# Layer 0's softmax maxima: one sequence of steps, half a pair ahead, in a fused two-layer decoder kernel

## The reference, cut to what matters

```
q = (x @ Wq).reshape(B, Nq, HEADS, DIM_HEAD)
k = (context @ Wk).reshape(B, context.shape[1], HEADS, DIM_HEAD)
v = (context @ Wv).reshape(B, context.shape[1], HEADS, DIM_HEAD)
sim = jnp.einsum('bihd,bjhd->bhij', q, k) * SCALE
attn = jax.nn.softmax(sim, axis=-1)
out = jnp.einsum('bhij,bjhd->bihd', attn, v)
```

## Time and profile before

| | |
|---|---|
| median of 3 runs | 1639.65 us (1639.27 to 1640.0) |
| the profiled execution | 1638.51 us, its span 1636.8 us |
| busy share of the span | PE 93%, DVE 79%, ACT 69%, POOL 30% |
| pair 0's maxima, alone | 59.6 to 125.1 us |
| slots of layer 0 | 130.0 to 1000.2 us |
| granted TensorE clock | 0.964 of full speed over the span |

### The profile page before, as it was taken

The page is one execution under the profiler, slowest core; times in us unless marked ns, Lnnn a source line. Parts: engine busy times, 40 slices in busy tenths (PEclk is TensorE's granted clock), DMA queues, the critical chain, the costliest instruction groups (busy, mean ns, idle before and its releaser), DMA issues.

```text
span 1636.8 us, 27033 instructions
## 1 busy us (share of the span) xinstructions
PE 1530.1 (93%) x9058; PEld 548.9 (34%) x9058; DVE 1286.3 (79%) x2319; ACT 1126.0 (69%) x1541; POOL 490.9 (30%) x488
## 2 busy tenths in 40 slices
PE   6889999999999999999999998899997979999986
PEld 4312333333333333333333223344444612222223
DVE  6898987879977779878789897877775666787766
ACT  6787777768877778777777786655554469676643
POOL 6303343334543334433300010345451012233100
PEclk9759999999999999999999998999999979999998
DMA  4000000000200000000010000111100000000000
GB/s 135 7 1 11 1 1 1 1 2 11 54 1 2 1 1 1 3 1 11 20 32 3 1 1 19 37 46 45 45 27 1 1 1 2 0 1 1 1 14 13
DMA packets 14834, 22.79 MB, mean 14 GB/s; under 512 B 1990, under 2 KB 11766, under 8 KB 14710
## 3 DMA queue, kind: packets, MB, share of 16 engines
q1 hardware_dynamic: 14710, 21.22, 4.6%
HBM read 20.69 MB, written 0.52 MB: 13 GB/s over the span
## 4 chain that ended last, share of the span: by engine, by line
PE 69%; issue 11%; DVE 9%; POOL 5%; ACT 4%; DMA 0%; POOLq 0%; SPq 0%; DVEq 0%; ACTq 0%
PE PS L2167 22%; PE PS L2153 15%; PE PS L2511 6%; PE PS L2199 5%; POOL WRK L734 5%; PE PS L2498 3%; DVE KNB L1382 3%; PE PS L2020 2%; PE PS L2012 2%; PE PS L2116 2%; PE PS L2540 2%; PE PS L2450 1%; PE PS L2435 1%; PE PS L2004 1%; ACT KNB L959 1%
## 5 line engine op out<-in xcount | busy, mean ns | idle before, releaser
L1382 DVE CUSTOM_DVE_ANT_0 KNB<-PS,KNB 128x512 f16<-128x512 f32 (+2 forms) x500 | 338.5, 690 | 152.4 <-PE PS L2199 106.9
L1432 DVE TENSOR_TENSOR WRK<-WRK 128x768 f32<-128x768 f32 (+3 forms) x400 | 425.2, 1063 | 15.3 <-ACT WRK L933 8.4
L933 ACT ACTIVATE WRK<-PS 128x1024 f32<-128x1024 f32 (+1 forms) x408 | 401.4, 1022 | 47.6 <-PE PS L2153 39.2
L2167 PE MATMUL PS<-WRK,V 128*64 128x512 f32 (+1 forms) x1632 | 395.7, 605 | 0.0
L708 POOL TENSOR_TENSOR WRK<-WRK 128x256 f32<-128x256 f32 x300 | 274.7, 916 | 395.6 <-ACT WRK L933 394.6
L959 ACT ACTIVATE KNB<-PS 128x512 f16<-128x512 f32 (+2 forms) x306 | 180.9, 591 | 77.8 <-PE PS L2199 77.2
L2344 PE MATMUL PS<-WRK,KNB 128*128 128x512 f16 x828 | 188.3, 381 | 7.1 <-POOL WRK L734 2.7
L2167 PEld LDWEIGHTS PS<-WRK,V 128*64 128x64 f32 (+1 forms) x1632 | 99.3, 136 | 192.7 <-issue 154.5
L2153 PE MATMUL PS<-KNB,KB 64*128 64x512 f16 (+1 forms) x1224 | 156.5, 377 | 0.0
L2153 PE MATMUL PS<-Q,KB 64*128 64x512 f16 (+1 forms) x1224 | 153.0, 377 | 0.0
L1162 ACT ACTIVATE WRK<-PS 128x1024 f32<-128x1024 f32 x100 | 102.4, 1024 | 51.1 <-PE PS L2498 47.6
(11 more groups left out here) (379 smaller groups left out, 1834.2 us busy)
## 6 DMA issues: line engine op xcount, KB each, us to landing
V<-in_moe_w_dram SPq DMA_DIRECT2D x44, 192.0 KB, 2.4
KNB<-in_ctx_fm_dram SPq DMA_DIRECT2D x6, 384.0 KB, 8.4
X<-in_ctx_fm_dram SPq DMA_DIRECT2D x12, 192.0 KB, 2.4
CTX<-in_ctx_fm_dram SPq DMA_DIRECT2D x6, 384.0 KB, 3.9
BW<-in_bit_w_dram SPq DMA_DIRECT2D x1, 960.0 KB, 9.8
PWK<-in_pair_w_dram SPq DMA_DIRECT2D x4, 192.0 KB, 2.8
XT<-in_x_fm_dram SPq DMA_DIRECT2D x1, 512.0 KB, 5.0
X<-in_x_tm_dram SPq DMA_DIRECT2D x1, 512.0 KB, 12.0
```

The source lines that it names most:

```text
L933: e.activation(PR[0:r, u % 2, b, :], bank(2 * b, 2 * b + 2, slice(0, r)), ACT.Exp).then_inc(S("exp"), 1)
L1382: return e.tensor_tensor_reduce(diffs, sums, diffs, 0.5, NEG, ALU.add, ALU.max, accum_out=out)
L1432: e.tensor_tensor(total, total, part, ALU.add).then_inc(S("acc"), 1)
L2167: ins = e.matmul(PS[h * HD:(h + 1) * HD, 4, :], V[0:r, j, h * HD:(h + 1) * HD], PR[0:r, unit_no(hf, i) % 2, b, h * HALF:(h + 1) * HALF], s ...
```

## The change

The steps become one sequence of 364 over the whole loop (`NSTEP`), 52 for each half from half 1 to half 7 (`NM`), each half's made on their own. Only half 0's maxima are found alone: 24 double steps and 2 short ones. The sequence starts in pair 0's slot 0 and goes through every slot, across the pairs' ends, two steps a slot with a third in slots 32, 34, 36, 38, 40, 42, 44, 48 and 50 of pairs 0 to 2 and in slots 3, 4 and 5 of pair 0. It ends in pair 3's slot 11, which has the last half step. The halves are complete in slots 24 and 47 of pair 0, 20 and 43 of pair 1, 15 and 39 of pair 2, and 11 of pair 3. In the slot behind each of these VectorE reduces that half's maxima and makes its two diagonal tiles, at the slot's start (`shifts`, which now holds what `diagonals` did).

A pair's `K16` chunks overwrite the ones before as soon as the half that reads them is through: slots `K16_AT` for `kd`, one later for `ks`. Queries, chunks and all else go through bank 5; `q` moves to slots 1 and 2. GpSimd also takes its quarter of the sums in half 6 (`POOL_HALVES`), makes the chain's first largest value ahead of that half and the second in its midst. The chain's first rounded copy goes to another tile (`KA[1]`), since `K16` is still read. The chain has one more empty item in front, so that its items stay in the same slots. The core of the diff:

```diff
-THIRD_M = (32, 36, 40, 44, 48)
...
+TILES_H = NT // 2
+STEPS = [[(c, [t], g) for c in range(NFULL) for t in range(TILES_H * u, TILES_H * u + TILES_H) for g in range(2)]
+         + [(NFULL, list(range(TILES_H * u + a, TILES_H * u + b)), g) for a, b in ((0, 3), (3, TILES_H)) for g in range(2)] for u in range(2)]
+NM = len(STEPS[0])
...
+ALONE0 = [(d, [t], g) for d in range(NDC - 1) for t in range(TILES_H) for g in range(2)] + [(NDC - 1, [0, 1, 2, 3], g)
+                                                                                     for g in range(2)]
...
+POOL_HALVES = 2 * PAIRS - 1
...
+NSTEP = NM * (2 * PAIRS - 1)
+WITH_VALUES = (32, 34, 36, 38, 40, 42, 44, 48, 50)
+THIRD_M = [(3, 4, 5) + WITH_VALUES] + [WITH_VALUES] * (PAIRS - 2) + [()]
+
+
+def first_step(p, s):
+    return min(2 * (p * SLOTS + s) + sum(len(x) for x in THIRD_M[:p]) + sum(t < s for t in THIRD_M[p]), NSTEP + 1)
...
+K16_AT = (6, 9, 13, 16, 20, 23, 25)
...
-        at[0] += [("wk", n), ("q", (n, 0)), ("q", (n, 1))]
-        at[1] += [("wv", n), ("kd", (n, 0)), ("ks", (n, 0))]
-        for c in range(1, NMC):
-            at[4 + 3 * c].append(("kd", (n, c)))
-            at[5 + 3 * c].append(("ks", (n, c)))
+        at[0].append(("wk", n))
+        at[1] += [("wv", n), ("q", (n, 0))]
+        at[2].append(("q", (n, 1)))
+        for c, k in enumerate(K16_AT):
+            at[k].append(("kd", (n, c)))
+            at[k + 1].append(("ks", (n, c)))
...
-CHAIN = [("none",)] * 2
+CHAIN = [("none",)] * 3
...
-        EMB = [KN[0].bitcast(BF16), KN[1].bitcast(BF16), KN[0].bitcast(BF16)]
+        EMB = [KA[1][:, :].bitcast(BF16), KN[1].bitcast(BF16), KN[0].bitcast(BF16)]
...
+            for hf in range(POOL_HALVES):
+                if hf == POOL_HALVES - 1:
+                    largest(0)
                 for i in range(NU):
                     for b in tiles_of(i):
                         add_up(hf, i, b)
-            for i in range(3):
-                e.wait_ge(S("ax"), i + 1)
-                e.partition_all_reduce(AM[:, i:i + 1], AX[:, i:i + 1], P, RED.max).then_inc(S("am"), 1)
+                    if hf == POOL_HALVES - 1 and i == CHAIN.index(("max", 1)) - 1:
+                        largest(1)
+            largest(2)
...
+            def shifts(hf, done, parts):
+
+                u, rows = hf % 2, slice(hf % 2 * NT, hf % 2 * NT + NT)
                 e.wait_ge(S("mx"), done)
-                link(e.tensor_reduce(NEGM[:, 0:rows], MXP[:, 0:rows, 0:parts], X, ALU.max, negate=True))
...
+                link(e.tensor_reduce(NEGM[:, rows], MXP[:, rows, 0:parts], X, ALU.max, negate=True))
+                if hf >= 2:
+                    e.wait_ge(S("sc"), tile_no(hf - 2, 0, 0) + 1)
+                for h in range(2):
+                    row = u * NT + h * TILES_H
                     ins = e.tensor_tensor(DIAG[:, h, 4 * u:4 * u + 4, :],
                                           ident16[:, :].unsqueeze(1).to_broadcast([P, 4, P]),
                                           NEGM[:, row:row + 4].unsqueeze(2).to_broadcast([P, 4, P]), ALU.mult)
                 ins.then_inc(S("diag"), 1)
...
-                    first, mid, last = split_steps(s) if p + 1 < PAIRS else ([], [], [])
-                    if s == SLOTS - 1 and p + 1 < PAIRS:
-                        shifts(micro_base(p + 1), NMC, 2 * NT)
-                        e.wait_ge(S("sc"), tile_no(2 * p, 0, 0) + 1)
-                        diagonals(0, 2, NT)
+                    first, mid, last = split_steps(p, s)
+                    if ready(p, s):
+                        shifts(ready(p, s), STEP0 + ready(p, s) * NM, NMC)
```

More of the change, by code:

```diff
@@ L93, in rows_of, with micro_steps, half_step, step @@
     return P if j < KT - 1 else TAIL
-THIRD_M = (32, 36, 40, 44, 48)
[L100 to L112, removed]
+NSTEP = NM * (2 * PAIRS - 1)
[3 more added lines that the diff above has]
+    return min(2 * (p * SLOTS + s) + sum(len(x) for x in THIRD_M[:p]) + sum(t < s for t in THIRD_M[p]), NSTEP + 1)
+def micro_steps(p, s):
+    return list(range(first_step(p, s), first_step(*divmod(p * SLOTS + s + 1, SLOTS))
+                      if p * SLOTS + s + 1 < PAIRS * SLOTS else NSTEP + 1))
+def half_step(m):
+    return 1 + m // NM, m % NM
+def step(m):
+    h, k = half_step(m)
+    return STEPS[h % 2][k]
+def half_done(p, s):
+    done = [m // NM for m in micro_steps(p, s) if m and m % NM == 0]
+    return done[0] if done else None
+def ready(p, s):
+    return half_done(*divmod(p * SLOTS + s - 1, SLOTS)) if p * SLOTS + s else None
+def split_steps(p, s):
+    steps = micro_steps(p, s)
+    return steps[:1], steps[1:-1], steps[1:][-1:]
 def inside(x):
     return x[0] == "dk"
-def micro_base(p):
-    return len(ALONE0) + NM * p
+STEP0 = len(ALONE0)
+K16_AT = (6, 9, 13, 16, 20, 23, 25)
 def items_of(p):
@@ L158 @@
             "bits": "bit_dve"}
[L159 to L166, removed]
+BANK5 = [x for p in range(PAIRS) for s in range(SLOTS) for x in ITEMS[p][s] if x[0] in FREED_BY]
+for _p in range(PAIRS - 1):
+    for _c, _k in enumerate(K16_AT):
+        _steps = [m for m in range(NSTEP) if step(m)[0] == _c]
+        _last = max(m for m in _steps if half_step(m)[0] == 2 * _p + 1)
+        _first = min(m for m in _steps if half_step(m)[0] == 2 * _p + 2)
+        assert first_step(_p, _k) > _last + 1 and first_step(*divmod(_p * SLOTS + _k + 2, SLOTS)) <= _first
 def freed(x):
@@ L1013, in _ @@
                         exp(hf, i, 1)
-                    magnitude(p, last)
+                    magnitude(last)
                     if i == 0 and hf:
@@ L1414, in _ @@
             max_alone(0, ALONE0, True)
-            shifts(len(ALONE0), NDC, 2 * NT)
-            for u in range(2):
-                diagonals(u, 2, NT)
+            shifts(0, STEP0, NDC)
             def add_up(hf, i, b):
@@ L1464, in add_out, with maximum @@
                 e.tensor_tensor(part, part, bank(5), ALU.add).then_inc(S("r_add"), 1)
-            def maximum(p, steps):
+            def maximum(steps):
                 for s in steps:
@@ L1583, in _ @@
                         add_up(*before, 0)
[L1584 removed]
+                    maximum(first)
                     if before[0] >= 0 and len(tiles_of(before[1])) > 1:
                         add_up(*before, 1)
[L1587 to L1588 removed]
+                    maximum(mid)
+                    maximum(last)
                     if p == 0 and s in BIT_AT:
@@ L2191, in project_out, with max_half @@
                 ins.then_inc(S("wo_ps"), 1)
-            def max_half(p, m, off, b, name):
-                c, tiles, g = STEPS[m]
+            def max_half(m, off, b, name):
+                c, tiles, g = step(m)
+                queries = QH[half_step(m)[0] // 2 % 2]
                 a, w = MCH[c]
```

99 lines of the change are left out of this document (41 added, 58 removed).

## The result

The changed kernel takes 1659.26 us in the median (1656.04 to 1663.18, four runs). The kernel before took 1639.46 in the median of the four runs beside it (1638.01 to 1640.0). The ratio is 1.0123 with an interval of 1.0099 to 1.0148. It is slower by 20 us, and outside the range of 1632 to 1650. The profiled execution is the fastest of the four, 1656.04 us with a span of 1654.3, 17.5 longer than before.

What follows compares the result with a forecast made beforehand. TensorE was taken to bound the slots, VectorE the maxima found alone. Added 34.7 us against 31.8 removed made 2.9 slower: 1641.4 for the profiled execution, 1642.8 in the runs' scale with 0.2 for GpSimd; range 1632 to 1650.

Steps and rivals of the forecast that it cites:

- rival 3: Half 6: GpSimd's second all-reduce holds it up; a recurring 5.8 us gap costs 0.2, counted; worse form has chance 0.06.
- the dearer form: Half 6: GpSimd's return to adds costs as much again, 5.5 us more, giving 1648; chance 0.06.
- (D): Seven reductions with diagonals at the start of slots with steps, ahead of VectorE's adds and maximum: 4.4 us, bounds 0 and 8.5.
- (E): Pair 3, slots 0 to 11: 22 steps beside the chain's rounding, bound passing to VectorE; 10.4 us, bounds 4.7 and 13.
- removed: Stage of maxima found alone: 24 of 48 double steps and half the short ones go, 31.8 us together.
- (A): Slots 0, 1 and 51 of pairs 0 to 2: two steps each, 3.9 us, plus 2.7 for ScalarE in slot 0.
- (B): Third steps in slots 34, 38, 42, 50 of three pairs: 12 at 0.78, 9.4 us; short steps moving, -0.3.
- (C): Third steps in slots 3, 4, 5 of pair 0 without values item: 1.4 us each, 4.2 in all, bounds 0.66 and 5.
- The 4.65: Pair 3, slots 5, 7, 8 and 10: VectorE's predicted time with a reciprocal, 4.65 us against 3.8 without.
- Rival 1: Whole kernel: steps fit, (D) swallowed by gaps, added time 19.9 us; 1627.8, or 1635.2 with half; chance 0.26.
- Rival 2: VectorE becomes the bound beyond pair 3: (D) 8.5, (E) 13, (A) 8; added 43 us, 1651; chance 0.12.
- the signs named in advance: Alone stage ending near 93; longer third-step slots and waits; pair 3's slots 4 to 10 above 4 us; GpSimd gap without late exponential.

Runs made afterwards that it cites:

- e2: Kernel before plus only GpSimd's part of the change: its quarter in half 6, two largest-value calls between additions; 1652.71 us, ratio 1.0083.
- e3: Changed kernel with GpSimd's first two all-reduces replaced by a copy of each partition's own value, additions kept; 1645.36 us, ratio 1.0037.
- The first experiment: Changed kernel with GpSimd's part undone: no share in half 6, largest-value calls behind all its layer 0 additions; 1648.08 us, ratio 1.0054.
- e7: Changed kernel without GpSimd's part, shifts spread, pair 0's third steps moved; then pair 3's normalization of half 5 later, second diagonals moved; 1637.64 us, ratio 0.9989.
- e9: On e7 with a pair 0 third step moved to slot 20: GpSimd adds in half 6's first 24 tiles, switches where nothing waits; 1634.79 us, ratio 0.9967.

## Why the prediction was wrong

**The step that failed** is the pricing of GpSimd's calls, in rival 3. The prediction had the place and the first gap of 5.80: one gap of some 6 us is hidden by a lead of 6.5, "0.2 us, which I count". That reckoning left the return to the additions at nothing unless proved dearer, gave the dearer form 0.06, and priced it at 5.5 us for one call, the second; the first, ahead of half 6, had no term. Measured: the return costs 7.0 us on top of 5.8, in both calls, and the total is 13.5 to 13.8 us (e2 and e3), 5.1 at the first call and 8.7 at the second.

"The trace has one such gap" was also a misreading. In the view that holds the 5.80, with nothing to wait for either, stands the way back. It is the first tensor_scalar behind the last of the three all-reduces, with only memsets and mask selections between them:

```profile
978.15 1.94 POOL L727 TENSOR_SCALAR BT<-SM 128x1 f32<-128x1 f32 x2 [7.53 <-issue]
```

It isn't a tensor_tensor, so it could not prove the price, but it was the nearest row, and it put 7.5 us where the sum had nothing. In the eleven kernels this gap is 6.90 to 8.03 us. With both gaps, 13.7 us of absence against the same lead of 6.5 gives 7.2 a call and 14.4 for two, 0.6 from what was found. That is close by luck: TensorE stood idle for 9.9 us only, 3.35 at the first call and 6.52 at the second in the longest waits, and the other 3.9 us are its clock behind the stalls, which had no term in any form.

The Trainium skill ("GPSIMD Engine Reference", 2.1 Instruction dispatch) has a load of about 6 us for the first call to a freshly loaded kernel. The traces agree with the size for the all-reduce, at 5.74 to 6.22 us, and show that "first" happens again at each switch. That a tensor_tensor behind it pays some 7 us, and a copy nothing, stands only in the runs. The traces also have a pair of records named MODIFY_POOL_CONFIG at each switch: in the changed kernel at 817.75, 0.2 us behind the last addition, at 824.13, when the copy ends and an addition comes up, and likewise at 902.86 and 909.25. The first experiment, with one switch, has one pair there, at 819.82.

**The rest of the sum was nearly right.** Without the 13.8 us the added time is 35.1 against 34.7 predicted, and the kernel would be within a few microseconds of before, as e3 is (1.0037). But two errors cancel in it, (D) too low and (E) too high:

| term | predicted | measured | where |
|---|---|---|---|
| removed | 31.8 | 31.5 | first exponential, 130.04 to 98.53 |
| (A) slots 0, 1, 51 | 6.6 | 6.9 | slots 0 to 2 of pair 0 +1.9, of the others +0.1 each, slot 51 +0.52 three times; 3.2 for the `K16` products that left slot 1 |
| (B) third steps with values | 9.1 | 10.3 | +0.82 in most, +1.20 in slot 50, -0.2 in the slots behind them |
| (C) slots 3, 4, 5 | 4.2 | 4.0 | +1.43, +1.27, +1.28 |
| (D) shifts | 4.4 | 6.7 | +1.70, +1.28, +1.52, +0.9, +0.85, +0.49 |
| (E) pair 3 | 10.4 | 6.7 | e3's half 6 |
| not foreseen | 0 | 0.5 | single slots; 3.8 less the 3.2 that belong to (A) |

(A) In pairs 1 and 2 slots 0 to 2 seem to take their extra steps for 0.1 us. No idle time of TensorE is filled there; it had next to none in pair 1's slot 0:

```profile
360.76:366.60 5.84, 5.64 (x36) 1.98 (x33) 1.06 (x3) 4.21 (x10) 1.12 (x2) 1.00 0.00 0
```

Products moved. The queries' went from slot 0 to slots 1 and 2, and so slot 0 falls to 4.08 us while the others rise. And the two products of the first `K16` chunk stood in slot 1 and stand in slots 6 and 7 now, with the later chunks pushed towards slot 26. Such a product costs 0.54 us (a slot of 4.24 against one of 3.70), so 1.1 a pair and 3.2 in all belong to (A) and show up in slots 6 to 25. This share is worked out from these two slot lengths, not run by itself.

(B) The timeline of TensorE in a slot with a new third step has exactly the shape of the earlier trace rows:

```profile
279.31 0.39 PE L2224 MATMUL PS<-KNB,Q 64*128 64x512 f16 x2
...
280.61 0.39 PE L2224 MATMUL PS<-KNB,Q 64*128 64x512 f16 x2 [0.25 <-DVE MXP L1413]
...
282.35 0.39 PE L2224 MATMUL PS<-KNB,Q 64*128 64x512 f16 x2
```

Again the middle step 1.30 behind the first and 0.25 idle. A duration read from the same kind of slot carries over.

(C) A third step without a values item, TensorE and then ScalarE's magnitude for its last step:

```profile
115.95 0.39 PE L2224 MATMUL PS<-KNB 64*128 64x512 f16 x2
...
117.25 0.39 PE L2224 MATMUL PS<-KNB 64*128 64x512 f16 x2 [0.27 <-DVE MXP L1413]
...
118.73 0.39 PE L2224 MATMUL PS<-KNB 64*128 64x512 f16 x2 [0.44 <-DVE MXP L1413]
```

```profile
117.95 0.59 ACT L989 ACTIVATE KNB<-PS 128x512 f16<-128x512 f32 x1
```

The magnitude begins 2.00 us behind the slot's first step (1.99 predicted), the last step 2.78 behind it (2.7). The profile puts the last step's wait down to VectorE's maximum and not to the magnitude; the two end within 0.04 us of each other, at 118.58 and 118.54, so the price came out right with either as the cause.

(D) was mis-sized where the prediction allowed for cover. In the slots with a third step the insertion of 2.0 us counts for 1.3 to 1.7; the 0.6 that short maxima were to give back did not show in pairs 0 and 2. In slots 25 and 21 it counts for 0.9, not 0.1 (slot 25's 0.9 also holds a `K16` product, for which the same slot of pairs 1 and 2 pays 0.22). Only slot 16 is right (0.5). Spreading the shifts gave back 4.2 us of the 6.7.

(E) The bound did pass to VectorE in part, as e7 shows and e9 with GpSimd's help: without the reciprocals slots 6, 8 and 9 fall from 4.37, 4.37 and 4.30 to 3.80, 3.70 and 3.56. Slots 4 to 10 sum to 27.8 us, where 29.6 was worked out and 1.0 added for the latency between engines. (The 4.65 is a slip: 3.8 and a reciprocal of 0.95 make 4.75.) The two lengths were of the right kind, 3.82 for 3.8 and 4.37 or 4.30 for 4.65, but only three slots are long (6, 8 and 9), slot 4 keeps TensorE's 3.70, and slot 10 takes 3.44. Slots 0 to 3 and 11 cost 1.8 and not 2.7. The addition for latency had no row behind it.

**The rivals.** Rival 1 (faster) did not happen in this kernel, and its condition, shifts swallowed by gaps, was false. Rival 2 was half true, with (D) high, (E) low and (A) as forecast. Of the signs named in advance most came: the alone stage ended at 92.5 (93), slots 3 to 5 took 5.0 to 5.1 (5.1), and GpSimd's gap was 5.78 (5 to 6). Two failed. Of pair 3's slots 4 to 10 only 6, 8 and 9 are above 4 us, and an exponential did come late behind GpSimd's call: that is the sign that names the 13.8 us.

## What to carry to other kernels

When an engine's stream gets a second kind of call, price the way there and the way back, and compare their sum with the lead of whoever waits; a lead that covers one is no cover for two. Look for the way back in the whole trace, behind any call of that kind. If TensorE waits behind the stall, add what its clock loses. If both kinds are needed, put the switch where nothing waits, and bring the old kind back with a tiny instruction ahead of time: here that turned GpSimd's help in half 6 from a loss of 11.1 us into a gain of 2.3. A short insertion on an engine that feeds another within the slot goes to the slot's end and in pieces; at its start it counted for 1.3 to 1.7 of its 2.0 us here, on an engine busy for three quarters of the time. And when work is moved as well as added, count the product at its old place too, or one slot looks free and others dear.
